# Moving the loads of the x tiles from GpSimd's queue, one tile ahead, to ScalarE's queue, at the head of their own iteration

## What is computed

```python
# attention: 16 query heads, 4 key/value heads, head size 128,
# sliding window 1024 plus 4 sink keys
x = x + layernorm(attention(layernorm(x), Wq, Wk, Wv, Wo))
# feed-forward: inner size 8192
x = x + layernorm(ffn(layernorm(x), w_gate_up, w_down))   # down(silu(gate) * up)
```

## Time and profile before

| | |
|---|---|
| median of 3 runs | 2309.29 us |
| lowest run | 2308.33 us |
| the profiled execution's own time | 2309.64 us |
| its span, first to last instruction of the slowest core (core 3) | 2307.8 us |
| spans of the eight cores | 2298.0 to 2307.8 us |
| mean granted TensorE clock, by core | 0.965 to 0.968 |
| TensorE matmuls busy | 2042.7 us (89%) |
| ScalarE busy | 951.3 us (41%) |
| VectorE busy | 446.9 us (19%) |
| GpSimd busy | 66.6 us (3%) |

### The profile page before, as it was taken

The page is one execution under the profiler, slowest core; times in us unless marked ns, Lnnn a source line. Parts: engine busy times, 40 slices in busy tenths (PEclk is TensorE's granted clock), DMA queues, the critical chain, the costliest instruction groups (busy, mean ns, idle before and its releaser), DMA issues.

```text
span 2307.8 us, 24002 instructions; the slowest of 8 cores (2298.0 to 2307.8 us)
## 1 busy us (share of the span) xinstructions
PE 2042.7 (89%) x9424; PEld 902.3 (39%) x9424; DVE 446.9 (19%) x592; ACT 951.3 (41%) x947; POOL 66.6 (3%) x87
## 2 busy tenths in 40 slices
PE   1767998987888886999999999999999999999971
PEld 1333443222222443444444444444444444444441
DVE  2121002543332441000111000111000210101234
ACT  4344345776664444333332333323333323333324
POOL 1100002400000000000000000000000000000000
PEclk9888999999999998999999999999999999999995
DMA  6421345501000333444553554644454635445525
GB/s 182 133 88 55 107 149 178 162 1 48 1 1 19 110 133 125 156 151 146 182 183 93 156 152 146 185 144 128 155 155 155 187 103 157 152 154 162 183 76 223
DMA packets 75566, 298.66 MB, mean 129 GB/s; under 512 B 8512, under 2 KB 8640, under 8 KB 69056
## 3 DMA queue, kind: packets, MB, share of 16 engines
q1 hardware_dynamic: 70848, 263.58, 36.3%
q0 software_dynamic: 4608, 33.56, 4.2%
HBM read 280.33 MB, written 16.78 MB: 129 GB/s over the span
## 4 chain that ended last, share of the span: by engine, by line
PE 78%; ACT 12%; issue 5%; DVE 3%; DMA 2%; ACTq 0%; POOL 0%; DVEq 0%; SPq 0%; POOLq 0%
PE ps_b L676 19%; PE ps_a L684 19%; PE ps_a L717 10%; PE ps_b L717 10%; ACT pt L459 6%; PE ps_a L410 3%; PE ps_a L450 3%; PE ps_a L592 3%; PE ps_a L308 2%; PE ps_b L592 2%; PE ps_a L323 2%; PE ps_b L410 1%; ACT h1t L378 1%; PE ps_b L323 1%; DMA wst<-wk_pe 1%
## 5 line engine op out<-in xcount | busy, mean ns | idle before, releaser
L249 ACT CAST wbf<-wst 128x1024 bf16<-128x1024 f32 x384 | 394.9, 1045 | 510.0 <-DMA wst<-wgu_pe 269.8
L676 PE MATMUL ps_b<-h2f,wbf 128*128 128x512 bf16 x2048 | 454.7, 380 | 4.0 <-ACT wbf L249 4.0
L684 PE MATMUL ps_a<-h2f,wbf 128*128 128x512 bf16 x2048 | 452.5, 379 | 0.0
L676 PEld LDWEIGHTS ps_b<-h2f,wbf 128*128 128x128 bf16 x2048 | 200.7, 98 | 247.4 <-issue 7.2
L684 PEld LDWEIGHTS ps_a<-h2f,wbf 128*128 128x128 bf16 x2048 | 200.5, 98 | 241.5
L696 DVE TENSOR_TENSOR a_sb<-silu_t,ps_a 128x1024 bf16<-128x1024 f32 x64 | 78.1, 1221 | 817.6 <-PE ps_a L684 792.4
L717 PE MATMUL ps_a<-a_sb,wbf 128*128 128x512 bf16 x1024 | 226.2, 379 | 5.9 <-DVE a_sb L696 5.9
L459 ACT ACTIVATE pt<-ps_a 128x2048 bf16<-128x2048 f32 x112 | 189.2, 1690 | 99.7 <-PE ps_a L450 99.7
L717 PE MATMUL ps_b<-a_sb,wbf 128*128 128x512 bf16 x1024 | 226.2, 379 | 0.0
L692 ACT ACTIVATE silu_t<-ps_b 128x1024 f32<-128x1024 f32 x64 | 65.5, 1024 | 340.2 <-PE ps_b L676 340.2
L477 DVE TENSOR_TENSOR pt<-pt,msk 128x2048 bf16<-128x2048 bf16 (+1 forms) x112 | 112.1, 1002 | 346.3 <-ACT pt L459 335.1
(11 more groups left out here) (106 smaller groups left out, 1111.0 us busy)
## 6 DMA issues: line engine op xcount, KB each, us to landing
wst<-wgu_pe SPq DMA_DIRECT2D x256, 512.0 KB, 4.4
wst<-wd_pe SPq DMA_DIRECT2D x128, 512.0 KB, 4.4
xt<-x_kv POOLq DMA_DIRECT2D x16, 1024.0 KB, 6.4
wst<-wq_pe SPq DMA_DIRECT2D x32, 512.0 KB, 4.5
wst<-wo_t SPq DMA_DIRECT2D x32, 512.0 KB, 4.5
xo<-x_kv POOLq DMA_DIRECT2D x8, 1024.0 KB, 7.2
wst<-wk_pe SPq DMA_DIRECT2D x8, 512.0 KB, 5.1
wst<-wv_t SPq DMA_DIRECT2D x16, 256.0 KB, 4.2
```

What stands on the lines that cost most here:

```text
L249: fn = [lambda g, d=dst_ap, sl=slot, n=n: g.copy(d, sl.ap()[:, 0:n])]
L676: fns.append(lambda t, c=c, ts=ts, rg=rg: t.matmul(PB[ts], wbf[rg].ap()[:, c * 128:(c + 1) * 128], h2f.ap()[:, c * 1024 + ts * 512:c * 102 ...
L684: fns.append(lambda t, c=c, ts=ts, ru=ru: t.matmul(pa[:, ts * 512:(ts + 1) * 512], wbf[ru].ap()[:, c * 128:(c + 1) * 128], h2f.ap()[:, c * ...
```

## The change

The sixteen loads of x tiles are issued from ScalarE's queue instead of POOL's. The load ahead of the loop is gone; iteration `idx` now queues the load of its own tile, `idx`, as the first thing that it queues. Buffers, their number, the sizes and the semaphores are the same. The other loads on POOL's queue (L578, L616) stay.

```diff
     def x_dma(idx):
         tb = TB_ORDER[idx]
         s = idx % 2
-        em.task("gpsimd",
+        em.task("scalar",
                 [lambda q, tb=tb, s=s: q.dma_start(out=xt[s].ap(),
                                                    in_=x_kv[tb * 128:(tb + 1) * 128, :])],
                 writes=[f"xt{s}"], stream=f"xt{s}")
 
-    x_dma(0)
     for idx, tb in enumerate(TB_ORDER):
         s = idx % 2
         par = idx % 2
         sx = STT[par][4]
-        if idx + 1 < 16:
-            x_dma(idx + 1)
+        x_dma(idx)
         if idx >= 6:
             while len(vback) > 1:
                 vproj(vback.pop(0))
```

## The result

The changed kernel takes 2352.04 us (median of 9 runs; before, in the same comparison, 2309.14 us of 10 runs). The ratio is 1.0187, with a 95% interval of 1.0176 to 1.0199: 43 us slower. The forecast was 2356.4 us and 0.60 for slower by over 2%; it came out just under 2%, inside the range of 2343 to 2379 us and inside the likeliest case's own range of 2346 to 2364.

What follows compares the result with a forecast made beforehand. TensorE was 78% of the chain, with the starting layernorm and projection loop the loose stage. Exposed loads 47.2, covered iterations +1 and start -1.4 gave +46.8 us on 2309.64: 2356.4 us, range 2343 to 2379.

Steps and rivals of the forecast that it cites:

- the likeliest case: Loads issued on ACT as the copy starts: 2356.4 us, own range 2346 to 2364, chance 59%.
- the ten exposed loads: Iterations 2, 3, 5, 7, 9 to 11, 13 to 15: no projections cover the load; period 13.4 us, 15.6 beside staging.
- the covered iterations: Iterations 4, 6, 8 and 12: four or five projections hide the load; 0, plus 1 us for low clock.
- The sum: All terms of the layernorm and projection loop added: 47.2 + 1 - 1.4 = 46.8 us slower.
- Point of issue (g): In exposed periods, from copy start to ACT's load issue: 0.1 us; issue at the copy's end would be 1.87 more.
- The row of ACT's sequencer: Profile row of standing waits over at 162.7 and 162.8: ACT's sequencer goes on past a computation still running.
- POOL's row: Profile row of POOL's load at 52.13, starting only when its two casts are finishing; pointed to the later issue.
- Landing (t): In exposed periods, from load issue to landing: 5.1 us alone, 7.3 beside staging.
- Transposes (a): In exposed periods, h1t to copy start: 4.2 us at the low clock, 3.4 to 3.5 only right behind a covered iteration.
- Start: Ahead of the second h1t: load 1 no longer beside load 0, -1.4 us together, bounds 0 and -5.5.
- POOL's queue: Wv casts no longer behind loads waiting for h1t: earlier, at most 1.1 us to gain, taken as 0.

Runs made afterwards that it cites:

- with h1t ahead: The kernel before, with bn_stats, Ln, Exp and the h1t activation queued ahead of an iteration's projections instead of behind them: ratio 0.9847 (0.9813 to 0.9881).

## Why the prediction was right

The mechanism held: the ten exposed loads, the issue at the copy's start and the covered iterations. The sum was 3.1 us too high against the trace (46.8 for 43.7), and the forecast of 2356.4 4.4 us too high against the median. Term by term, h1t to h1t on core 3:

| iterations | expected | measured |
|---|---|---|
| 2 and 3, beside wv staging | 31.2 (+16.8) | 30.61 (+16.2) |
| 5 | 13.4 (+6.4) | 13.94 (+7.0) |
| 7 | 12.7 (+2.7) | 12.40 (+2.4) |
| 9 to 11 | 39.4 (+11.1) | 38.65 (+10.3) |
| 13 to 15 | 40.2 (+10.2) | 39.33 (+9.4) |
| covered: 4, 6, 8, 12 | +1 | +1.2 (24.55, 24.71, 24.93, 23.87) |
| start, until the second h1t | -1.4 | -2.75 (37.05 for 39.80) |
| sum | +46.8 | +43.7 |

- **Point of issue (g).** Expected 0.1 us behind the copy's start; measured 0.01 to 0.02. The row of ACT's sequencer was the right one to go by, and POOL's row did not carry over to ACT. This choice carried the most: with the issue at the copy's end the kernel took 22 us more.
- **Landing (t).** Expected 5.1 alone and 7.3 beside staging; measured 4.8 to 5.0 for most, 5.7 for load 5, and 6.9 for loads 2 and 3, beside staging. The terms of 7, 9 to 11 and 13 to 15 came out 1.9 us too high together, 1.2 of it by t and most of the rest by g.
- **Transposes (a).** At the low clock in most exposed periods as expected (copy 4.2 us behind h1t). At the high clock (3.4) only behind 6 and 8; behind the covered iterations 4 and 12 it was 4.2 and 4.0. The prediction's words gave 3.4 to 3.5 behind every covered iteration, but its sum took 4.2 for 5 and 13, and the sum was the better of the two.
- **Covered iterations.** The +1 for a longer spell at the low clock was met by 1.2, but it isn't spread: iteration 8 alone gave 1.1 (transposes 1.86 us for 1.05, the first projection 5.4 for 5.1).
- **Start.** The mis-sized term: -2.75 for -1.4. The sum moved only the second cast. But load 1 had slowed the first wk pieces too: the first cast starts at 10.83, and it had ended at 14.08, so had started at 13.04; with load 1 back beside load 0 it starts at 14.20. The first h1t came 3.1 us earlier, and load 1 beside the next wk pieces took 0.4 back (expected 0.7).
- **POOL's queue.** The wv casts did come earlier: before, the first projection of iteration 6 had waited 0.4 us for one. A slower start of TensorE took half of that back (24.71 for 24.94); the sum had 0.
- **The chances.** 0.60 for slower by over 2% rested on 46.8 being a little over 46.2; the 2% line (2355.5 us) lies at the middle of the sum's own range, not a little below it. The start's error (1.4) would have put the sum under that line by itself, and so would the other terms together (1.7). Which side it fell on was close to even, and the 0.60 was on the wrong one. The 2% is also not what this comparison can just tell from no change, as the prediction has it: the interval is 0.12% wide to either side.

By the rule cited there (the Trainium skill, Perfetto Trace Analysis, the per-engine timelines) a sequencer executes such a DMA itself. The trace agrees: in all sixteen iterations but the first the issue is at the copy's start, with the copy still running. By the first-byte figures of the Trainium skill, DMA: Bandwidth & Descriptors (specification table), ACT's path would be 0.4 us quicker than POOL's, an estimate from 1 and 0.6 us; the traces show 4.8 to 5.0 for 5.1 to 5.4, about that, and 0.2 of it is the shorter issue itself (0.33 us for 0.53).

## What to carry to other kernels

On ScalarE a DMA was issued when the engine's sequencer passed the last standing wait ahead of it, not when the data were wanted and not when the computation ahead of it ended; ask what that wait is for. (On POOL the loads behind a cast went out only as the cast was ending, so this doesn't carry over to every engine.) Moving a prefetch to a busy engine's queue, or writing it later in the program, may each cost next to nothing and both together much. And when a transfer is hidden, look for what does set the beat: here it was a small eviction that stood ahead of the next Ln, and taking it behind was worth about as much (some 44 us) as the exposed loads had cost.

## What the runs showed of the hardware

- ACT computed and issued at once: a 0.33 us issue 0.01 to 0.02 us into a 1.87 us copy, for fifteen of the sixteen loads of the changed kernel. POOL did not: its load at 52.13 and load 3 at 43.94 above were issued as a cast was ending.
- One 1 MB load took 4.8 to 5.0 us from ACT's queue and 5.1 to 5.4 from POOL's for most loads late in the loop, with nothing else under way on that core; beside staging 6.9 and 6.7 to 8.6.
- In some executions all the late loads of single cores took about 1 us longer, on either queue: with h1t ahead, 5.9 to 6.6 us on cores 0, 5 and 6 and 5.0 to 5.6 on the other five; with the loads on ACT's queue one tile ahead, 5.3 to 6.2 us on cores 3 and 6 and 4.6 to 5.1 on most others. No run shows why.
- The granted clock has a third level. In the profiled execution with h1t ahead core 0 had the full clock in a stretch of projections, and core 5 of the other die 0.81 in every 6 us of it that were looked at, so this is no mean of full and half, the only two levels named ahead of the prediction. Core 0, then core 5, 42 us from nearly the same point of the program:

```profile
104.00:146.00 42.00, 34.82 (x219) 17.71 (x218) 13.63 (x29) 25.26 (x28) 2.64 (x5) 1.00 0.29 101
...
107.00:149.00 42.00, 39.31 (x198) 18.26 (x197) 11.83 (x25) 22.25 (x26) 2.11 (x4) 0.81 0.26 90
```

The profile has 219 matmuls of core 0 in it and 198 of core 5. Why core 5 was held there isn't shown by any run.
